# A six-stage decoder on one core: the tail of each row normalisation on GpSimd, two expert operands joined, one clamp left out

## The reference, cut to what matters

```python
def _layernorm(x, axis=-1, eps=1e-05):
    m = jnp.mean(x, axis=axis, keepdims=True)
    v = jnp.var(x, axis=axis, keepdims=True)
    return (x - m) / jnp.sqrt(v + eps)
...
    x = x + _L0_attn_ref(_layernorm(x), ...)            # 16 heads, causal
    x = x + _L0_xattn_ref(_layernorm(x), ctx, ctx)      # 32 query heads on 8 kv heads
    x = x + _L0_ffn_ref(_layernorm(x), gate, up, down)  # block-quantised operands
    x = x + _L1_attn_ref(_layernorm(x), ...)            # state-space scan
    x = x + _L1_xattn_ref(_layernorm(x), ctx, ...)
    x = x + _L1_ffn_ref(_layernorm(x), W, gate_w, A, B) # linear plus routed low-rank experts
```

## Time and profile before

| | |
|---|---|
| runs | 1609.81, 1601.79, 1609.12 us, median 1609.12 |
| the profiled execution's own time | 1603.94 us |
| its span, first to last instruction | 1602.2 us |
| PE busy | 1361.3 us, 85% |
| DVE busy | 1332.5 us, 83% |
| ACT busy | 1037.2 us, 65% |
| POOL busy | 428.2 us, 27% |
| mean granted PE clock | 0.939 of full speed |

### The profile page before, as it was taken

One profiled execution on the slowest core, in us unless ns is written; L12 is line 12 of the kernel. 1 busy time (PEld: TensorE's weight loads), 2 busy tenths in 40 slices (PEclk: granted clock), 3 DMA queues, 4 the chain that ended last, 5 costly groups with the idle time before them and its releaser, 6 DMA issues.

```text
span 1602.2 us, 32850 instructions
## 1 busy us (share of the span) xinstructions
PE 1361.3 (85%) x13068; PEld 745.7 (47%) x13068; DVE 1332.5 (83%) x1965; ACT 1037.2 (65%) x1884; POOL 428.2 (27%) x495
## 2 busy tenths in 40 slices
PE   3778878879899999898978767879999998999986
PEld 2454535344445453444443333446555555555643
DVE  6988989979879888887798899888788888978743
ACT  3244365465673865765695769886899788989431
POOL 1432141132240422321331240241222313122310
PEclk9697989799999999999999988889999999999988
DMA  6313122200201111002120003011020211101020
GB/s 223 93 54 93 34 68 68 74 15 1 75 15 41 36 41 42 21 22 54 63 89 28 1 1 132 20 41 44 2 71 13 59 39 33 41 5 44 2 81 27
DMA packets 54201, 76.24 MB, mean 48 GB/s; under 512 B 8480, under 2 KB 23840, under 8 KB 53536
## 3 DMA queue, kind: packets, MB, share of 16 engines
q1 hardware_dynamic: 54048, 74.14, 16.2%
HBM read 38.98 MB, written 9.44 MB: 30 GB/s over the span
## 4 chain that ended last, share of the span: by engine, by line
PE 47%; DVE 29%; ACT 10%; issue 7%; POOL 4%; DMA 1%; SPq 1%; ACTq 0%; DVEq 0%; POOLq 0%
PE bank L200 16%; DVE mix_NM L1079 4%; PE bank L1178 4%; PE bank L534 3%; DVE ssm_HS L1537 2%; PE bank L542 2%; PE bank L522 2%; PE bank L992 2%; PE bank L1204 2%; PE bank L557 2%; DVE ffn_m L1133 2%; PE bank L977 2%; POOL attn_P L737 2%; PE bank L495 1%; DVE ffn_Z L1142 1%
## 5 line engine op out<-in xcount | busy, mean ns | idle before, releaser
L1052 ACT ACTIVATE mix_P<-bank 128x512 f32<-128x512 f32 x256 | 142.3, 604 | 50.6 <-PE bank L977 50.2
L1079 DVE TENSOR_REDUCE mix_NM<-bank 128x2 f32<-128x512 f32 x256 | 162.8, 682 | 11.2 <-PE bank L952 10.4
L737 POOL TENSOR_SCALAR_AFFINE_SELECT cross_P<-cross_P 128x256 f32<-128x256 f32 x128 | 90.5, 717 | 272.9 <-ACT cross_P L642 272.4
L1296 POOL TENSOR_TENSOR ffn_room<-ffn_room 128x512 f32<-128x512 f32 x64 | 89.9, 1406 | 263.9 <-ACT ffn_room L1235 167.0
L1537 DVE TENSOR_TENSOR_SCAN ssm_HS<-ssm_DA,ssm_DD 128x1024 f32<-128x1024 f32 x64 | 150.3, 2348 | 10.1 <-ACT ssm_DD L1488 5.5
L737 POOL TENSOR_SCALAR_AFFINE_SELECT attn_P<-attn_P 128x256 f32<-128x256 f32 x128 | 89.6, 713 | 243.7 <-ACT attn_P L642 243.7
L1485 ACT ACTIVATE ssm_DA<-ssm_Z,A_T 128x255 f32<-128x255 f32 x256 | 110.9, 498 | 3.1 <-DVE ssm_HS L1537 2.7
L642 ACT ACTIVATE attn_P<-bank 128x384 f32<-128x384 f32 x128 | 63.8, 498 | 63.1 <-PE bank L523 62.7
L642 ACT ACTIVATE cross_P<-bank 128x384 f32<-128x384 f32 x128 | 62.6, 489 | 50.9 <-PE bank L523 50.5
L1543 DVE TENSOR_TENSOR ssm_HS<-ssm_HS,ssm_CS 128x1024 f32<-128x1024 f32 x64 | 82.0, 1281 | 0.9
L1460 ACT ACTIVATE ssm_Z<-bank 128x512 f32<-128x512 f32 x128 | 72.2, 599 | 13.4 <-PE bank L1374 12.8
(11 more groups left out here) (410 smaller groups left out, 4043.3 us busy)
## 6 DMA issues: line engine op xcount, KB each, us to landing
attn_stack<-attn_P SPq DMA_DIRECT2D x96, 128.0 KB, 2.4
cross_stack<-cross_P SPq DMA_DIRECT2D x96, 128.0 KB, 2.4
ffn_room<-f_gate SPq DMA_DIRECT2D x4, 1024.0 KB, 5.3
XR<-x SPq DMA_DIRECT2D x8, 512.0 KB, 6.8
ffn_room<-f_up SPq DMA_DIRECT2D x4, 1024.0 KB, 5.6
ffn_room<-f_down SPq DMA_DIRECT2D x4, 1024.0 KB, 4.9
x_mid<-XR SPq DMA_DIRECT2D x8, 512.0 KB, 3.0
XR<-x_mid SPq DMA_DIRECT2D x8, 512.0 KB, 3.7
```

The source lines that it names most:

```text
L737: nc.gpsimd.affine_select(out=diagonal, in_=diagonal, compare_op=ALU.is_ge, fill=0.0, base=0, pattern=[[0, 2], [1, P]], channel_multiplier ...
L1052: nc.scalar.activation(self.p[h % 8], bank[b4[h % 2]][:, :], ACT.Exp, scale=HD2 ** -0.5).then_inc(s["p_ready"], 1)
L1079: nc.vector.tensor_reduce(self.nm[:, t, 16 * i + 2 * g:16 * i + 2 * g + 2], bank[b4[u % 3]][:, :].rearrange("p (c k) -> p c k", c=2), AX.X ...
L1296: nc.gpsimd.tensor_tensor(self.inter[q % 2][:, 512 * (g % 2):512 * (g % 2) + 512], self.sg[g % 2], self.up[g % 2], ALU.mult).then_inc(s["i ...
```

## The change

1. `dve_moments` ends with the two `bn_aggr`, each of which now raises `var_ready`. The DVE wait behind them and the two tiny DVE operations are gone. `pool_root` waits for a count of two for each row, adds EPS (new POOL instruction), waits for its own result, takes the power, computes minus the mean (new POOL instruction), waits for both and multiplies.
2. `dve_quantise` gets an argument `bounded`. With it the clamp of the block maxima and the wait behind it are left out. The call on the normalised row uses it, the four calls on the gated product don't.
3. The two expert operands `f_a` [128, 4, 128] and `f_g` [128, 4, 8] become one, `f_ag` [128, 4, 136], of the same total size. The two groups of 12 matmuls for each token tile become one group of 12 with 136 columns. The loader fills the two column ranges from the same two sources.

The strings of turns are the same, and so is what each turn stands for.

```diff
                 for t in range(TT):
-                    own(nc.vector.bn_aggr(self.mv[:, t, :], self.stats[:, t, :]))
+                    nc.vector.bn_aggr(self.mv[:, t, :], self.stats[:, t, :]).then_inc(self.var_ready, 1)
+
+            def pool_root(self, pool, own, n):
+                pool.wait_ge(self.var_ready, TT * (n + 1))
+                own(nc.gpsimd.tensor_scalar(self.var[:], self.mv[:, :, 1], EPS, None, ALU.add))
                 own.wait()
-                own(nc.vector.tensor_scalar(self.negative[:], self.mv[:, :, 0], -1.0, None, ALU.mult))
-                nc.vector.tensor_scalar_add(self.var[:], self.mv[:, :, 1], EPS).then_inc(self.var_ready, 1)
-
-            def pool_root(self, pool, own, n):
-                pool.wait_ge(self.var_ready, n + 1)
                 own(nc.gpsimd.tensor_tensor(self.rstd[:], self.var[:], minus_half[:], ALU.pow))
+                own(nc.gpsimd.tensor_scalar(self.negative[:], self.mv[:, :, 0], -1.0, None, ALU.mult))
                 own.wait()
                 nc.gpsimd.tensor_tensor(self.shift[:], self.negative[:], self.rstd[:], ALU.mult
...
-            def dve_quantise(self, dve, own, src):
+            def dve_quantise(self, dve, own, src, bounded=False):
...
-                own(nc.vector.tensor_scalar(m, m, TINY, HUGE, ALU.max, ALU.min))
-                own.wait()
+                if not bounded:
+                    own(nc.vector.tensor_scalar(m, m, TINY, HUGE, ALU.max, ALU.min))
+                    own.wait()
...
-                self.dve_quantise(dve, own, self.xn[:, :, :].rearrange("p t d -> p (t d)"))
+                self.dve_quantise(dve, own, self.xn[:, :, :].rearrange("p t d -> p (t d)"), bounded=True)
...
-                    product(bank[b][:, at:at + ER], [(xt(k, t), self.f_a.view(lambda t_: t_[:, k, :]))
-                                                     for k in range(DC)])
-                    last = product(bank[b][:, at + ER:at + ER + E], [(xt(k, t), self.f_g.view(lambda t_: t_[:, k, :]))
-                                                                     for k in range(DC)])
+                    last = product(bank[b][:, at:at + ER + E], [(xt(k, t), self.f_ag.view(lambda t_: t_[:, k, :]))
+                                                                for k in range(DC)])
...
-            f_a = split_weight(l1, "f_a", [P, DC, ER])
-            f_g = split_weight(l1, "f_g", [P, DC, E])
+            f_ag = split_weight(l1, "f_ag", [P, DC, ER + E])
...
-                (whole(f_a), chunk(G["A"])), (whole(f_g), chunk(G["g"])), (whole(f_b), G["B"])],
+                (f_ag.view(lambda t_: t_[:, :, 0:ER]), chunk(G["A"])),
+                (f_ag.view(lambda t_: t_[:, :, ER:ER + E]), chunk(G["g"])), (whole(f_b), G["B"])],
```

More of the change, by code:

```diff
@@ L1585, in build, with __init__ @@
         class Experts:
-            def __init__(self, st, b, x, f_w, f_a, f_g, f_b, first_choice):
+            def __init__(self, st, b, x, f_w, f_ag, f_b, first_choice):
                 self.b, self.x = b, x
-                self.f_w, self.f_a, self.f_g, self.f_b, self.first_choice = f_w, f_a, f_g, f_b, first_choice
+                self.f_w, self.f_ag, self.f_b, self.first_choice = f_w, f_ag, f_b, first_choice
                 self.xn = sb(st, "lora_XN", [P, TT, D])
@@ L1817, in build @@
                               context_ready=lambda n: (ct_in, 32 * (n - B + 1)), before=attn)
-            lora = Experts(l1, 7, row1, f_w, f_a, f_g, f_b, first_choice)
+            lora = Experts(l1, 7, row1, f_w, f_ag, f_b, first_choice)
             weights_a = Loader("l1a", [
```

## The result

The kernel after takes 1616.16 us (median of 8 runs, 1612.69 to 1622.54), the kernel before 1608.12 (8 runs, 1601.79 to 1609.81): a ratio of 1.0058, 95% interval 1.0037 to 1.008. It is slower by 8 us. 1605 was predicted, with 1594 to 1614 as range: wrong in sign, and outside the range. The profiled execution of after took 1616.27 us with a span of 1614.5; that of before 1603.94 and 1602.2, so these two spans lie 12 us apart where the medians lie 8.

The account below looks back on a forecast made before the run. No single engine was taken to bound it: the chain passes between PE and DVE. The terms -5.3 - 1.5 - 2.2 + 5.1 = -3.9 us gave a median of 1605.2, predicted as 1605, range 1594 to 1614.

Parts of the forecast that it names:

- 1a: Two small DVE operations leaving the norms: 5.0 us of chain pieces plus 0.28 of gaps in 14 norms, gain 5.3 us.
- even: In four chain norms, aggregates to power: 0.36 us now against 0.34 after (signal 0.08, addition 0.19, wait 0.07).
- 1b: Two added POOL instructions in each norm, between bn_aggr and rstd_ready: cost 0.8 + 1.4 + 2.9 = 5.1 us.
- 4 x 0.19: In four chain norms through DVE and POOL, the negation delays the multiplication by 0.19 us each: 0.8 us.
- 0.45 ... 1.4 us: In three norms with POOL itself late on the chain, addition, wait and negation count whole, 0.45 us each: 1.4 us.
- 2 of the 7 new gaps: New gaps between dependent POOL instructions in 7 chain norms: two lost to DVE, costing 2.9 us.
- 2.2 + 1.1: The 2.2 is POOL's fixed part of the added cost: 0.8 us in four norms and 1.4 in three.
- the gaps go to DVE: Rival: POOL's four-step tail loses its turn to DVE twice in a norm, 12 lost turns, +12, 1621 us; chance 0.12.
- the aside on a factor of 2: With POOL elementwise work 2 times slower, each new instruction would be 0.33 us and the added POOL cost some 1.4 dearer.
- The upper bound of the sum: New POOL instructions at 0.69 us each and all 7 new gaps lost at 1.45: cost 19.3 us, net +10.3.
- Parts 2 and 3: Clamp off the chain in 7 input calls, 1.5 us; joined expert matmuls in 8 groups on the chain, 2.2 us.

Follow-up runs that it names:

- the first experiments: Against the kernel before, each in 5 rounds beside it: only the tail moved to GpSimd, 1622.22 us; only the clamp and expert-operand parts, 1605.51 us.
- the version without the two: The changed kernel with its two added GpSimd instructions (EPS addition, negation of the mean) left out: 1596.51 us, ratio 0.9919 to the kernel before.
- the other version with fills: The changed kernel without its two added GpSimd instructions, with two small fills of scratch in place of each: 1601.76 us, ratio 0.9962 to the kernel before.
- the version with fills: The kernel before plus four small GpSimd fills of scratch in each norm's tail, two ahead of the power and two behind: 1613.98 us, ratio 1.0036.

## Why the prediction was wrong

**1a, relief of VectorE: right in mechanism, too small.** -5.3 predicted, -9.0 measured (parts 2 and 3 with and without VectorE's two instructions, none added on GpSimd). That measurement also holds the shorter way into GpSimd, which the prediction booked as "even" in 1b: 0.36 - 0.08 = 0.28 us in 4 norms, 1.1 us. The rest, 2.6 us, I put down to relief off the chain, at which I had put no value; no run separates it. The next VectorE instruction starts 0.06 us behind the second aggregate (1100.67 + 0.25 = 1100.92, and 1100.98), as foreseen.

**1b, what is added to POOL: the step that failed.** +5.1 predicted; with the 1.1 us just named, 6.2 gross. 19.7 and 22.3 measured. Three things in it, by size:
- *Which norms count.* It charged the instructions to the 7 norms where GpSimd was on the chain before ("4 x 0.19", "0.45 ... 1.4 us", "2 of the 7 new gaps"). After the change GpSimd's tail is on the chain in 15 norms with 53.4 us, against 7 with 14.6 before. Of the 8 new ones, 4 had VectorE's part on the chain before (mix at 109 us, ffn at 830, cross at 1228, lora at 1235), and 4 had neither part on it (attn at 334, mix at 798, ssm at 804, cross at 1372). These had little slack on the side of GpSimd: once the tail is 0.64 us longer, or 2 us with a lost turn, the chain goes that way instead. At 0.4 the 31 us of added length alone are worth some 12 us, an estimate, where the prediction had 2.2 + 1.1 for it.
- *Lost turns.* 2.9 us were put down for 2 turns. The tails have 20 us of added waiting, and 23 norms over 2 us in place of 10; at 0.4 it is 8 us, and with the 12 for length the 20 that were measured. Here "the gaps go to DVE" was the right mechanism for the smaller part, at a chance of 0.12. It named cross and lora norms; the worst single place was a mix norm beside weight quantisation (3.54 us at 318 before, 8.08 at 323 after).
- *The price of one.* 0.19 to 0.20 taken, 0.22 and 0.24 measured, and a wait of 0.07 to 0.08 at each of two more steps: 0.64 a norm by the shortest tails. An undisturbed norm, from the end of the aggregates to the end of the shift, is 0.08 + 1.61 = 1.69 us; 1.52 had been predicted, 1.32 is before. A small error. (In the aside on a factor of 2, the prediction left out the longer addition in the four norms: 1.9 us dearer, not 1.4.)

The upper bound of the sum had the same flaw: it took each price at its highest, and still for 7 norms only (+19.3 for 1b, net +10.3). It came near the measured cost by luck, by a price of 0.69 that is three times the real one. The range then stopped at 1614, short of this end of the sum at 1619, and the measured 1616 lies between the two.

One reading of the rows was off as well. The VectorE negation of the earlier trace rows ended at 257.95, which is 0.9 us after the GpSimd addition beside it (254.57 + 2.46 = 257.03). It ended with the instruction behind that, a fill: `256.97 0.95 POOL L1104 MEMSET mix_P<- 128x1024 f16 x1`. That VectorE waits for GpSimd stands.

**Parts 2 and 3:** -3.7 predicted, -2.7 (-0.6 to -5.0 by the interval) measured together. The 12 matmuls of 136 columns, in the timeline of PE:

```profile
1123.39 0.22 PE L200 MATMUL bank<-f_ag_h,lora_XH 128*128 128x136 f16 x1
...
1124.04 0.22 PE L200 MATMUL bank<-f_ag_h,lora_XL 128*128 128x136 f16 x1
```

Eleven steps in 0.65 us, 59 ns each, as foreseen (56 to 60).

**The clock**, of which the prediction says nothing. Within the 8 runs of after, time and granted clock go together: 1612.69 at 0.936, 1616.27 at 0.932, 1622.54 at 0.926, about 10 us for 0.01. At the same clock of 0.936 the kernels stand at 1612.7 and 1608.2 us (each by a line through its runs, for the kernel before those beside the first experiments). So some 4.5 of the 8 us are there without it, and 3.5 come with a clock that is lower on the mean, as at 240 us where it fell behind a gap that the tail had made. That all of the 3.5 has this cause is argued, not shown. By such lines the 19.7 us of the two instructions would be some 13, and the 22.3 some 18 (an estimate: the version without the two ran at 0.939 to 0.945). So a part of the 0.36 to 0.46 us for a microsecond of tail comes with the clock too.

**Net:** -9.0 - 2.7 + 19.7 = +8.0 us, each term a difference of two measured versions.

## What to carry to other kernels

When an edit lengthens a step that others wait for, don't count only the places where that step is on the chain now: count all places, at a share of their sum (about 0.4 here; the share of places through which the chain passed on any engine was near it), because a chain that has a near alternative moves to it. The move from one engine to another is two edits, relief at the sender and length at the receiver; price each alone, and look for a version that has some of the first without the second, as one instruction for two on VectorE was. A tiny instruction on GpSimd in a dependent series is dear when VectorE is kept in long instructions: its work was 0.24 us, its mean up to 0.86.

## What the runs showed of the hardware that was not expected

- Arithmetic of two elements on GpSimd (0.22 to 0.24 us alone) waits out a VectorE instruction of 1 to 2.3 us in some norms, up to 2.17 us in one place. It did so beside VectorE instructions that read only SBUF tiles (27 of 96), and beside none that reduces or reads a PSUM bank (37 of 96).
- A fill of 16 elements took 0.10 to 0.13 us in 190 of 192 uses in the same positions, and two in a row take 0.05 us each of the chain. It did not wait for VectorE's scan or its products of two tiles. It did wait in 2 uses here for VectorE's TENSOR_SCALAR L1154, and in 4 of 192 in the other version with fills (up to 0.94 us beside `ffn_room<-ffn_room 128x2048 int32`, a TENSOR_SCALAR as well); beside another TENSOR_SCALAR, of float32, it did not.
- One idle stretch of TensorE of about 5 us was followed by 5 us at a granted clock of 0.50. In the version with fills, where it did 2.75 us of work in the same window (after: 0.13), the window behind it was granted 0.66:

```profile
235.00:240.00 5.00, 2.75 (x32) 0.99 (x30) 4.90 (x5) 4.71 (x11) 4.68 (x15) 1.00 0.00 0
240.00:245.00 5.00, 4.58 (x66) 2.77 (x69) 3.89 (x5) 1.66 (x4) 3.85 (x6) 0.66 0.01 3
```

- The run-to-run spread of one kernel on one core goes with the clock: in the 8 runs of after, 10 us of time for 0.01 of granted clock.
